# Second attention layer: one zero-finding instruction for two heads, score banks as a ring, softmax sums through a column of ones

## The chip, the cores and the metric

The kernel runs on one core of one Trainium2 chip. The metric is the device time of one execution in microseconds; times of runs are medians. The engines are named as in the profile: PE (TensorE matmul), PEld (its weight loads), DVE (VectorE), ACT (ScalarE), POOL (GpSimd) and SP (SyncE, which issues DMAs). Each engine takes its instructions in the order written, and semaphores tie the engines together.

## What is computed

Two transformer layers over x of shape 2 x 1024 x 128, each with attention and a feed-forward part, with layer norms and residual sums around each. The change touches the attention of the second layer, and the placing of scores in PSUM in both:

```
Q, K, V = split(x @ qkv.T)            # 16 heads of 8, rotary applied to Q and K
scores = Q K^T / sqrt(8)
scores = scores * lower_triangle
scores = where(scores == 0.0, -inf, scores)
attn = softmax(scores)
out = (attn @ V) @ wo.T
```

So in the second layer every score that is exactly zero is masked, which takes an instruction of its own on DVE. The first layer has 16 heads of 64 and a plain causal mask.

## The kernel before

**Items and steps.** An attention is a list of items (turn, batch, tile of 128 queries, head). In the second layer (k = 1) a turn covers 4 heads of the 16, and there are 4 turns of 64 items, 256 items in all. A turn has two halves of 32 items: batch 0 with query tiles qt = 0 to 7, then batch 1 with qt = 7 to 0, four heads of a tile after one another (a group). An item of tile qt has n = (qt + 1) * 128 keys, so 128 of the 256 items have at most 512 keys. `Attention` plans this; every engine walks the same list in a loop of its own, with these steps for item i:

- PE (`attention`, `values` in the tensor block): the scores of item i into PSUM (L1067, and L1071, which adds the causal mask); where item i - 4 ends a group, the product with V of that group (L1032), preceded by a transpose of the inverted sums (L1021); then the transposes of the probabilities of item i - 2 (L1091), for which it waits for the exponential of item i - 2. Then comes the score of item i + 1.
- DVE (`mask`, `maximum`): Zb, which is -1e30 where a score is zero (L787), then Sm, scores plus Zb with their row minimum (nmax) in one instruction and a read of the accumulator (L801). Once a group it also writes reciprocals of the sums (L769), spreads them over the columns (L776) and multiplies values by them (L759).
- ACT: the copies of the transposed probabilities PSUM to SBUF (L554), the exponential from Sm with the row sum in its accumulator (L574), and once a group a copy of the transposed factors (L536).

**PSUM.** Scores have four banks of 512 columns, as two tensors of two banks; item i writes tensor i % 2, whatever its size. Hence the score of item i waits for item i - 2 (`pe.wait_ge(a["p"] if k == 0 else a["mx"], i - 1)`).

**DMA.** SP loads Q and K of the next turn (`stacks`, 18 DMAs for each batch) once the last scores of a half are done. In the first layer the softmax factors are spread once a half turn: SP writes them to DRAM and reads them back broadcast over partitions (`spread`), and POOL multiplies 128 x 1024 values by them (L498).

**After attention** PE multiplies by wo1 (L1230, 16 tiles of 128 tokens), and norms and the last feed-forward part follow.

The steps as in the code:

```
for i in range(plan.n + QUEUED + 1):
    ... scores of i ...
    if plan.ends_group(i - QUEUED):
        values(k, plan.group(i - QUEUED), i)
    if i < plan.n + 2:
        if i >= 2:
            pe.wait_ge(a["p"], i - 1)
        ... transposes of item i - 2 ...
```

## Time and profile before

| | us |
|---|---|
| runs, median (lowest to highest) | 1345.51 (1344.99 to 1348.77) |
| the profiled execution's own time | 1347.31 |
| its span, first to last instruction | 1345.5 |
| busy: PE, DVE, ACT, POOL | 1147.0, 938.8, 850.0, 122.8 |
| first-layer attention, about | 42 to 640 |
| second-layer attention, about | 875 to 1281 |

Busy time says how much of the span an engine had an instruction at work; neighbours on one engine overlap by some tens of ns in these records, so start to start is the measure of what one costs in a row. "Idle before" names what ended the idle time of that engine.

### The profile page before, as it was taken

The page shows a single profiled execution, that of the slowest core. Times are in us where ns is not written, and L with a number is a line of the kernel's source. Part 1 is how long each engine was busy: PE and PEld are TensorE (multiplying, and loading weights), DVE is VectorE, ACT ScalarE, POOL GpSimd, SP SyncE.
Part 4 walks back from the last instruction along what each step waited for, and adds up shares of the span by engine and source line. Part 5 has one row for each costly group of instructions (what it writes and reads, how often), then busy time and mean ns, then how long its engine had stood idle before and what let it go on. Part 6 is the DMA issues. An engine that isn't in the chain of part 4 may idle for free.

```text
span 1345.5 us, 28730 instructions
## 1 busy us (share of the span) xinstructions
PE 1147.0 (85%) x10458; PEld 856.4 (64%) x10458; DVE 938.8 (70%) x2353; ACT 850.0 (63%) x1996; POOL 122.8 (9%) x105
## 2 busy tenths in 40 slices
PE   3699999989898989989989995188888888888886
PEld 1476767767676767767957773055655655656674
DVE  4466666666566666666543337589999899999953
ACT  2466666656666666665044332389989889999923
POOL 1600000000000000000400005100000000000033
PEclk9899999999999999999979997679999999999998
DMA  4212222221212222220100000422022022020001
GB/s 115 71 40 64 54 64 70 65 70 36 75 51 52 55 68 66 64 64 18 48 5 17 17 11 1 129 37 37 2 37 37 2 37 37 2 37 2 2 1 32
DMA packets 29672, 56.77 MB, mean 42 GB/s; under 512 B 4538, under 2 KB 14674, under 8 KB 29410
## 3 DMA queue, kind: packets, MB, share of 16 engines
q1 hardware_dynamic: 28738, 53.43, 17.4%
q8 instruction: 82, 1.34, 0.4%
q10 hardware_dynamic: 800, 1.57, 0.4%
q14 instruction: 52, 0.43, 0.1%
HBM read 25.49 MB, written 4.33 MB: 22 GB/s over the span
## 4 chain that ended last, share of the span: by engine, by line
PE 40%; DVE 26%; issue 18%; ACT 11%; DMA 3%; SPq 1%; POOL 1%; ACTq 0%; DVEq 0%; POOLq 0%
DVE Zb L787 9%; PE pT L1091 7%; PE pO L1032 7%; PE pS L1067 6%; ACT probs L574 4%; PE pS L1153 4%; DVE nmax L797 4%; PE pT L1165 3%; DVE Sm L801 3%; ACT PT L554 2%; PE pS L1114 2%; PE pT L994 2%; PE pT L998 2%; DVE Kl L737 1%; PE pS L1250 1%
## 5 line engine op out<-in xcount | busy, mean ns | idle before, releaser
L1091 PE MATMUL pT<-cst,probs 128*128 128x128 f32 x2304 | 374.0, 287 | 84.8 <-ACT probs L574 54.0
L1091 PEld LDWEIGHTS pT<-cst,probs 128*128 128x128 f32 x2304 | 248.9, 142 | 180.6 <-ACT probs L574 120.2
L574 ACT ACTIVATE probs<-pS,nmax 128x128 f32<-128x128 f32 (+7 forms) x256 | 190.1, 743 | 191.4 <-DVE nmax L797 157.9
L554 ACT COPY PT<-pT 128x512 f32<-128x512 f32 (+3 forms) x597 | 275.1, 483 | 12.8 <-PE pT L1091 11.3
L797 DVE TENSOR_REDUCE nmax<-pS 128x1 f32<-128x128 f32 (+7 forms) x256 | 192.1, 751 | 93.3 <-PE pS L1071 92.0
L1032 PE MATMUL pO<-PT,V 128*64 128x128 f32 (+1 forms) x4608 | 229.8, 276 | 7.9 <-issue 4.0
L574 ACT ACTIVATE probs<-Sm,nmax 128x128 f32<-128x128 f32 (+7 forms) x256 | 199.3, 778 | 28.6 <-DVE nmax L801 22.4
L787 DVE TENSOR_SCALAR Zb<-pS 128x128 bf16<-128x128 f32 (+7 forms) x256 | 192.8, 753 | 21.6 <-PE pS L1071 21.5
L1032 PEld LDWEIGHTS pO<-PT,V 128*64 128x64 f32 (+1 forms) x4608 | 179.9, 113 | 27.4 <-issue 6.5
L801 DVE CUSTOM_DVE_ANT_0 Sm<-pS,Zb 128x128 f32<-128x128 f32 (+7 forms) x256 | 193.4, 756 | 4.5
L1067 PE MATMUL pS<-Kh,Qs 128*128 128x512 f32 (+2 forms) x384 | 174.7, 459 | 7.1 <-DMA Kl<-Kl 6.9
L833 DVE COPY PT<-pT 128x512 f32<-128x512 f32 (+3 forms) x171 | 87.8, 514 | 74.0 <-PE pT L1091 70.7
L1067 PE MATMUL pS<-KS,QS 72*128 72x512 bf16 (+3 forms) x384 | 107.1, 333 | 33.2 <-DMA KS<-split 29.9
L1067 PE MATMUL pS<-Kl,Qs 128*128 128x512 f32 (+2 forms) x384 | 131.5, 346 | 0.0
L1071 PE MATMUL pS<-causalb,identb 128*128 128x128 bf16 x512 | 116.7, 228 | 0.0
L1067 PEld LDWEIGHTS pS<-Kh,Qs 128*128 128x128 f32 x384 | 75.3, 196 | 28.7 <-issue 22.9
L464 POOL TENSOR_TENSOR rstd<-rstd,power 128x4 f32<-128x4 f32 x32 | 32.8, 1025 | 622.1 <-DVE rstd L694 621.6
L498 POOL TENSOR_TENSOR attnT<-attnT,wq_t 128x1024 f32<-128x1024 f32 x16 | 37.9, 2369 | 550.0 <-DMA wq_t<-factors 505.0
L1067 PEld LDWEIGHTS pS<-Kl,Qs 128*128 128x128 f32 x384 | 74.8, 195 | 20.2 <-issue 16.0
L1071 PEld LDWEIGHTS pS<-causalb,identb 128*128 128x128 bf16 x512 | 50.4, 98 | 54.6 <-issue 33.3
L614 ACT ACTIVATE hT<-pS,b1e 128x512 f32<-128x512 f32 x64 | 43.8, 687 | 59.0 <-PE pS L1153 58.9
L994 PE MATMUL pT<-xnT,w0s 128*128 128x512 f32 x128 | 73.7, 663 | 8.5 <-DVE Ql L733 7.8
(177 smaller groups left out, 1270.9 us busy)
## 6 DMA issues: line engine op xcount, KB each, us to landing
Qs<-Ql SPq DMA_DIRECT2D x32, 256.0 KB, 3.7
Kh<-Kh SPq DMA_DIRECT2D x32, 256.0 KB, 3.6
Kl<-Kl SPq DMA_DIRECT2D x32, 256.0 KB, 4.6
wq_t<-factors SPq DMA_DIRECT2D x32, 256.0 KB, 4.0
QS<-split SPq DMA_DIRECT2D x72, 64.0 KB
KS<-split SPq DMA_DIRECT2D x72, 64.0 KB
w0s<-in_w SPq DMA_DIRECT2D x8, 192.0 KB, 4.8
split<-parts SPq DMA_DIRECT2D x2, 768.0 KB, 3.5
```

The source lines that it names most:

```text
L554: nc.scalar.copy(PT[:, g % 2, h, k0 * P:(k0 + nk) * P], pT[r % TBANKS][:, 0:nk * P])\
L574: nc.scalar.activation(probs[:, i % NPROB, 0:n], src[:, 0:n], ACT.Exp, bias=nmax[:, i % 4:i % 4 + 1], scale=sign, accum_out=total).then_in ...
L787: nc.vector.tensor_scalar(Zb[:, i % NMASK, 0:n], pS[i % 2][:, 0:n], 0.0, MASKED, ALU.is_equal, ALU.mult).then_inc(a["z"], 1)
L797: nc.vector.tensor_reduce(nmax[:, i % 4:i % 4 + 1], pS[i % 2][:, shift(k, qt):shift(k, qt) + n], AX.X, ALU.max, negate=True).then_inc(a["m ...
L801: nc.vector.tensor_tensor_reduce(Sm[:, i % NMASK, 0:n], pS[i % 2][:, 0:n], Zb[:, i % NMASK, 0:n], -(DH1 ** -0.5), 3e38, ALU.add, ALU.min, ...
L833: nc.vector.tensor_copy(PT[:, gg % 2, hh, k0 * P:(k0 + nk) * P], pT[r % TBANKS][:, 0:nk * P])\
L994: return nc.tensor.matmul(p, w0s[:, what, :], xnT[:, b * S + j * BANK:b * S + (j + 1) * BANK], start=True, stop=True)
L1032: m = nc.tensor.matmul(pO[rows, 0:P], v, PT[:, g % 2, h, kt * P:(kt + 1) * P], start=(kt == 0), stop=(kt == qt), skip_group_check=True)
L1067: nc.tensor.matmul(pS[i % 2][:, (off + c0) * P:(off + c1) * P], lhs, keys[:, b, h, c0 * P:c1 * P], start=(n == 0), stop=(n == len(rhs) - 1 ...
L1071: nc.tensor.matmul(pS[i % 2][:, (off + qt) * P:(off + qt + 1) * P], identb[:, :], causalb[:, :], start=False, stop=True).then_inc(a["s"], 1)
L1091: m = nc.tensor.transpose(pT[r % TBANKS][:, kt * P:(kt + 1) * P], probs[:, item % NPROB, (k0 + kt) * P:(k0 + kt + 1) * P], ident)
L1153: nc.tensor.matmul(bank[u % 4], w1s[:, buf, f * P:(f + 1) * P], xnT[:, j * BANK:(j + 1) * BANK], start=True, stop=True).then_inc(up_done, 1)
```

## The change

Four parts:

- `mask` runs once for two heads where n is at most 512: one instruction over 2 x n scores in two neighbouring banks. It waits until both items have their scores. Larger items keep one instruction each.
- Score banks are a ring: an item of at most 512 keys takes one bank, a larger one two, and the score of an item waits for the last item that held its banks (`place_scores`). This holds for both layers. The wait becomes i - 4 for most small items of the second layer, stays i - 2 for large ones, and is i - 2 or i - 3 in the first layer.
- V of the second layer gets a column of ones before each head's 8 columns, so that row 0 of each head's 32 rows of the output is the sum. The accumulator of the exponential, the reciprocals, the spreading copy, PE's transpose of factors and DVE's multiplication go. ACT's copy takes the values themselves, to attn1T.
- Once a half turn SP moves the sums to DRAM and back as 128 x 32, DVE inverts them (at item 16 of the next half, `invert_sums`), SP moves them out and in broadcast with four DMAs, and POOL multiplies 128 x 1024 values. PE waits for the last of these halfway through wo1.

The steps' distances stay: `lag` is 2 for both layers, so the transposes of item i - 2 still come in step i.

```diff
+        self.lag, self.queued, self.nprob = lag, lag + 2, lag + 1
...
+    def place_scores(self):
+        self.bank_of, self.after, last, at = [], [], [-1] * 4, 0
+        for i, (_, _, qt, _) in enumerate(self.items):
+            size = -(-(qt + 1) * P // BANK)
+            at = 0 if at + size > 4 else at
+            self.bank_of.append(at)
+            self.after.append(max(last[at:at + size]))
+            last[at:at + size] = [i] * size
+            at = (at + size) % 4
...
+    def masks(self, i):
+        if self.items[i][2] >= TPB:
+            return 1
+        return 2 if i % 2 == 0 else 0
...
+        V1 = at(32, "V1", [P, NT, HEADS, DH1 + 1])
+        rsb1 = at(42, "rsb1", [P, S])
+        sums = at(46, "sums", [P, HPG * S // P])
...
+            def spread1(half):
+                g, b = divmod(half, B)
+                sp.wait_ge(A[1]["n"], (half + 1) * ST)
+                sp.dma_start(sums_row[half, :, :], attn1T[0:P:HEAD_ROWS, b, g, :]).then_inc(sums_out, 16)
+                sp.wait_ge(sums_out, 16 * (half + 1))
+                sp.dma_start(sums[:, :], sums_row[half, :, :].rearrange("h (j i) -> (h j) i", i=HPG * S // P)).then_inc(sums_in, 16)
+                sp.wait_ge(sums_inverted, half + 1)
+                sp.dma_start(factors1[half, :, :].rearrange("h (j i) -> (h j) i", i=HPG * S // P), sums[:, :]).then_inc(factors1_out, 16)
+                sp.wait_ge(factors1_out, 16 * (half + 1))
+                if half >= 1:
+                    sp.wait_ge(rescaled1, half)
+                for h in range(HPG):
+                    sp.dma_start(rsb1[h * HEAD_ROWS:h * HEAD_ROWS + DH1 + 1, :],
+                                 factors1[half, h:h + 1, :].to_broadcast([DH1 + 1, S])).then_inc(factors1_in, 16)
...
+            for half in range(G1 * B):
+                values = attn1T[:, half % B, half // B, :]
+                pool.wait_ge(factors1_in, 16 * HPG * (half + 1))
+                pool.tensor_tensor(values, values, rsb1[:, :], ALU.mult).then_inc(rescaled1, 1)
...
+            def values_out(a, g):
+                c, b, qt = L[1].order[g]
                 act.wait_ge(a["o"], g + 1)
-                nc.scalar.copy(rs[:, g % 2, :], pO[:, P:2 * P]).then_inc(a["rs"], 1)
+                nc.scalar.copy(attn1T[:, b, c, qt * P:(qt + 1) * P], pO[:, 0:P]).then_inc(a["n"], 1)
...
                 def mask(i):
-                    n = (plan.items[i][2] + 1) * P
-                    dve.wait_ge(a["s"], i + 1)
+                    n, heads = (plan.items[i][2] + 1) * P, plan.masks(i)
+                    dve.wait_ge(a["s"], i + heads)
                     if i >= NMASK:
-                        dve.wait_ge(a["p"], i - NMASK + 1)
+                        dve.wait_ge(a["p"], i - NMASK + heads)
...
+                    half, at_half = divmod(i, plan.per // B)
+                    if k == 1 and at_half == 16 and half >= 1:
+                        invert_sums(half - 1)
...
-                        if i >= 2:
-                            pe.wait_ge(a["p"] if k == 0 else a["mx"], i - 1)
+                        if plan.after[i] >= 0:
+                            pe.wait_ge(a["p"] if k == 0 else a["mx"], plan.after[i] + 1)
...
-                    if i < plan.n + 2:
-                        if i >= 2:
-                            pe.wait_ge(a["p"], i - 1)
+                    if i < plan.n + plan.lag:
+                        if i >= plan.lag:
+                            pe.wait_ge(a["p"], i - plan.lag + 1)
...
+            pe.wait_ge(rescaled1, G1 * B - 1)
             for n in range(NT):
+                if n == ST:
+                    pe.wait_ge(rescaled1, G1 * B)
```

Order on DVE in the second layer, where items of 256 keys give way to 384, before (Zb and Sm are written from the scores pS; a1_s counts scores done, a1_p exponentials, a1_z masks):

```order
L787 TENSOR_SCALAR Zb<-pS 128x384 [waits a1_p,a1_s]
L759 TENSOR_TENSOR attn1T<-pO,rs 128x128 [waits a1_rs]
L801 ISA Sm,nmax<-pS,Zb 128x384 [waits a1_z]
L801 ISA nmax 128x1
L787 TENSOR_SCALAR Zb<-pS 128x384 [waits a1_p,a1_s]
L769 RECIPROCAL rden<-den 128x4 [waits a1_p]
L801 ISA Sm,nmax<-pS,Zb 128x384 [waits a1_z]
L801 ISA nmax 128x1
L776 COPY rdb<-rden 128x128 [waits a1_rd1]
```

and with the change, at the same place:

```order
L836 TENSOR_SCALAR Zb<-pS 128x2x384 [waits a1_p,a1_s]
L849 ISA Sm,nmax<-pS,Zb 128x384 [waits a1_z]
L849 ISA nmax 128x1
L849 ISA Sm,nmax<-pS,Zb 128x384 [waits a1_z]
L849 ISA nmax 128x1
L836 TENSOR_SCALAR Zb<-pS 128x2x384 [waits a1_p,a1_s]
```

One Zb stands ahead of two Sm, and waits for two scores; the three once-a-group instructions are gone.

Order on PE at that place with the change (a1_mx counts Sm done, a1_cp_act ACT's copies; pT holds transposes):

```order
L1113 MATMUL pS<-KS,QS 128x384 [waits a1_mx]
L1117 MATMUL pS<-causalb,identb 128x128
L1137 MATMUL pT<-cst,probs_77 128x128 [waits a1_cp_act,a1_p]
L1137 MATMUL pT<-cst,probs_77 128x128
L1113 MATMUL pS<-KS,QS 128x384 [waits a1_mx]
L1117 MATMUL pS<-causalb,identb 128x128
L1137 MATMUL pT<-cst,probs_77 128x128 [waits a1_cp_act,a1_p]
L1137 MATMUL pT<-cst,probs_77 128x128 x2
```

It is the order of before (there L1067, L1071, L1091, with the same waits): between the scores of two items stand the transposes of an earlier one, which wait for an exponential. What moved is only the count of a1_mx that a score waits for.

## Rows read from the trace of the kernel before

**Rows 1.** The page: the span.

```profile
span 1345.5 us, 28730 instructions
```

**Rows 2.** Stretches: PE, PEld, DVE, ACT, POOL busy, PEclk, DMA share, GB/s.

```profile
900.00:1000.00 100.00, 85.51 (x1048) 59.72 (x1047) 97.63 (x242) 92.62 (x242) 0.00 (x0) 1.00 0.19 25
975.00:980.00 5.00, 3.68 (x48) 2.27 (x45) 4.42 (x29) 4.71 (x24) 0.00 (x0) 1.00 0.27 45
```

**Rows 3.** Groups by form, 875 to 1285 us: busy us, mean ns | idle before.

```profile
L787 DVE TENSOR_SCALAR Zb<-pS 128x1024 bf16<-128x1024 f32 x32 | 39.0, 1219 | 0.0
...
L574 ACT ACTIVATE probs<-Sm,nmax 128x512 f32<-128x512 f32 x32 | 23.4, 733 | 2.9 <-DVE nmax L801 1.3 <-PE pT L1091 0.9
L801 DVE CUSTOM_DVE_ANT_0 Sm<-pS,Zb 128x512 f32<-128x512 f32 x32 | 22.0, 689 | 0.6
...
L787 DVE TENSOR_SCALAR Zb<-pS 128x256 bf16<-128x256 f32 x32 | 13.5, 421 | 1.6 <-PE pS L1071 1.5
L574 ACT ACTIVATE probs<-Sm,nmax 128x128 f32<-128x128 f32 x32 | 12.9, 404 | 0.7 <-issue 0.2
```

**Rows 4.** Timeline, 990 to 992 us, 512 keys: start, duration, engine, line.

```profile
990.07 0.72 ACT L574 ACTIVATE probs<-Sm,nmax 128x512 f32<-128x512 f32 x1 [0.28 <-PE pT L1091]
...
990.70 0.19 ACT L574 ACTIVATION_READ_ACCUMULATOR probs<-Sm,nmax 128x1 f32 x1
...
990.94 0.66 PE L1091 MATMUL pT<-cst,probs 128*128 128x128 f32 x4 [0.48 <-ACT probs L574]
991.21 0.08 DVE L801 DVE_READ_ACCUMULATOR2_ANT nmax<- 128x1 f32 x1
...
991.38 0.72 ACT L574 ACTIVATE probs<-Sm,nmax 128x512 f32<-128x512 f32 x1
...
991.65 0.22 PE L1071 MATMUL pS<-causalb,identb 128*128 128x128 bf16 x1
```

**Rows 5.** Timeline, 1271 to 1278 us, 256 and 128 keys.

```profile
1271.37 0.22 PE L1071 MATMUL pS<-causalb,identb 128*128 128x128 bf16 x1
...
1271.63 0.42 DVE L787 TENSOR_SCALAR Zb<-pS 128x256 bf16<-128x256 f32 x1 [0.19 <-PE pS L1071]
...
1276.94 0.33 PE L1091 MATMUL pT<-cst,probs 128*128 128x128 f32 x1
...
1277.16 0.22 PE L1071 MATMUL pS<-causalb,identb 128*128 128x128 bf16 x1
```

**Rows 6.** Timeline of DVE: first Zb of 512 keys down, first of 640 up.

```profile
960.59 0.69 DVE L787 TENSOR_SCALAR Zb<-pS 128x512 bf16<-128x512 f32 x1
...
994.01 0.82 DVE L787 TENSOR_SCALAR Zb<-pS 128x640 bf16<-128x640 f32 x1
```

**Rows 7.** Timeline of DVE, items of 1024 keys.

```profile
919.24 1.22 DVE L801 CUSTOM_DVE_ANT_0 Sm<-pS,Zb 128x1024 f32<-128x1024 f32 x1
...
924.17 1.22 DVE L801 CUSTOM_DVE_ANT_0 Sm<-pS,Zb 128x1024 f32<-128x1024 f32 x1
...
926.58 1.23 DVE L801 CUSTOM_DVE_ANT_0 Sm<-pS,Zb 128x1024 f32<-128x1024 f32 x1
...
929.06 1.22 DVE L801 CUSTOM_DVE_ANT_0 Sm<-pS,Zb 128x1024 f32<-128x1024 f32 x1
```

**Rows 8.** Groups by form, 100 to 600 us, first layer: a score's matmul.

```profile
L1067 PE MATMUL pS<-Kh,Qs 128*128 128x512 f32 x129 | 68.1, 528 | 0.0
```

**Rows 9.** Line 971 on DVE: ns min/median/max, both operands in SBUF.

```profile
L971 DVE TENSOR_TENSOR rot<-rot x4: 1212/1217/3285, 836.5 to 856.8; 128x1024 f32<-128x1024 f32 x4
```

**Rows 10.** Timeline of SP and of POOL at the first layer's last half.

```profile
639.05 0.31 SPq L379 DMA_DIRECT2D factors<-factorsT  x1
640.45 1.08 SPq L386 DMA_DIRECT2D wq_t<-factors  x2
...
645.02 2.35 POOL L498 TENSOR_TENSOR attnT<-attnT,wq_t 128x1024 f32<-128x1024 f32 x1 [17.19 <-DMA wq_t<-factors]
```

**Rows 11.** Chain that ended last, 1270 us to the end.

```profile
1280.97 16.19 PE pS L1230 x128
```

More of the change, by code:

```diff
@@ L55 @@
 STACK = PARTS * PARTS * DH1
+HEAD_ROWS = P // HPG
 KIB = 1024
@@ L133, in order_for_dve, with scores @@
             self.done_by[step]["dve"] = count
+    def place_scores(self):
[7 more added lines that the diff above has]
+            at = (at + size) % 4
+        self.masked_by, count = [], 0
+        for i in range(self.n):
+            count += self.masks(i) > 0
+            self.masked_by.append(count)
+    def masks(self, i):
+        if self.items[i][2] >= TPB:
+            return 1
+        return 2 if i % 2 == 0 else 0
+    def scores(self, pS, i, k0, nk):
+        start = self.bank_of[i] * BANK + k0
+        return pS[:, start:start + nk]
     def project(self, step, c, b, u):
@@ L560, in exponential @@
                         n, g = (qt + 1) * P, plan.group(i)
-                        if i >= NPROB:
-                            act.wait_ge(a["t"], plan.round_of[i - NPROB] + 1)
+                        if i >= plan.nprob:
+                            act.wait_ge(a["t"], plan.round_of[i - plan.nprob] + 1)
                         half, at_half = divmod(i, plan.per // B)
+                        if k == 0 and half >= 2 and at_half == 0:
+                            act.wait_ge(dens_inverted, half - 1)
@@ L573, in exponential @@
-                        src, sign = (pS[i % 2][:, shift(k, qt):], 1.0) if k == 0 else (Sm[:, i % NMASK, :], -1.0)
-                        nc.scalar.activation(probs[:, i % NPROB, 0:n], src[:, 0:n], ACT.Exp,
-                                             bias=nmax[:, i % 4:i % 4 + 1], scale=sign,
-                                             accum_out=total).then_inc(a["p"], 1)
-                for i in range(plan.n + QUEUED + 1):
-                    if k == 1 and plan.ends_group(i - QUEUED):
-                        factors_out(a, plan.group(i - QUEUED))
+                            nc.scalar.activation(probs(k, i)[:, 0:n], plan.scores(pS, i, shift(k, qt), n), ACT.Exp,
+                                                 bias=nmax[:, i % 4:i % 4 + 1],
+                                                 accum_out=den0[:, half % 2, h, qt:qt + 1]).then_inc(a["p"], 1)
+                        else:
+                            nc.scalar.activation(probs(k, i)[:, 0:n], Sm[:, i % NMASK, 0:n], ACT.Exp,
+                                                 bias=nmax[:, i % 4:i % 4 + 1], scale=-1.0).then_inc(a["p"], 1)
@@ L581, in attention @@
+                for i in range(plan.n + plan.queued + 1):
+                    if k == 1 and plan.ends_group(i - plan.queued):
+                        values_out(a, plan.group(i - plan.queued))
                     if k == 0:
@@ L744, in copy_turned, with invert_sums, attention @@
                 nc.vector.tensor_copy(factorsT[:, :], pO[0:HPC * ST, P:2 * P]).then_inc(turned_copied, 1)
-            def attention(k, put):
+            def invert_sums(half):
+                dve.wait_ge(sums_in, 16 * (half + 1))
+                nc.vector.reciprocal(sums[:, :], sums[:, :]).then_inc(sums_inverted, 1)
+            def attention(k):
                 a, plan = A[k], L[k]
@@ L818, in attention @@
                         maximum(i)
-                    if summed:
-                        spread(plan.group(i - 2))
+                    half, at_half = divmod(i, plan.per // B)
+                    if k == 1 and at_half == 16 and half >= 1:
+                        invert_sums(half - 1)
                     for r in plan.dve_at[i]:
@@ L975, in _ @@
             nc.vector.memset(pO[:, 0:P], 0.0).then_inc(pO_cleared, 1)
-            attention(1, lambda g, b, qt: attn1T[:, b, g, qt * P:(qt + 1) * P])
+            nc.vector.memset(rsb1[:, :], 0.0)
+            nc.vector.memset(V1[:, :, :, 0:1], 1.0).then_inc(pO_cleared, 1)
+            attention(1)
+            invert_sums(G1 * B - 1)
             norm_stage(3, y_tile, y_ready(3))
@@ L1018, in values @@
                     turn(g // ST - 1)
-                if k == 1:
-                    pe.wait_ge(a["rd"], g + 1)
-                    nc.tensor.transpose(pO[:, P:2 * P], rdb[:, g % 2, :], ident)
-                for e2, done in plan.done_by[i - QUEUED + 2].items():
+                for e2, done in plan.done_by[i - plan.queued + plan.lag].items():
                     if done:
@@ L1037, in attention @@
                 a, plan = A[k], L[k]
-                for i in range(plan.n + QUEUED + 1):
+                for i in range(plan.n + plan.queued + 1):
                     if i < plan.n:
@@ L1276 @@
     wo1 = np.zeros((HPG, P // HPG, G1, D), np.asarray(L1_attn_wo).dtype)
-    wo1[:, 0:DH1] = np.asarray(L1_attn_wo).T.reshape(G1, HPG, DH1, D).transpose(1, 2, 0, 3)
+    wo1[:, 1:DH1 + 1] = np.asarray(L1_attn_wo).T.reshape(G1, HPG, DH1, D).transpose(1, 2, 0, 3)
     arrays = {
```

118 lines of the change are left out of this document (50 added, 68 removed).

## The prediction

> **What bounds the kernel now.** I read the page first. The span is 1345.5 us [rows 1]; the profiled execution took 1347.31 us, 1.8 us more than its span, and the median of the runs is 1345.51 us. The sums below are made against 1347.31, and the result is then taken 1.8 us lower, to stand against the median. What a measurement of this kernel can tell from no change is about 0.3%, or 4 us.
>
> Second, the stretches. In a 100 us stretch of the second layer's attention DVE is busy 97.63, ACT 92.62 and PE 85.51 [rows 2]. So DVE sets the pace there, ACT is close behind, and PE has slack. The change takes work from DVE and from ACT, which sounds like a gain. But less work on the engine that sets the pace helps only while the inputs of its next instruction are there when it comes to it. So the third view is the timeline, for how long the path takes from one Sm through ACT and PE back to a Zb.
>
> That path exists because of the order on PE: between two scores stand the transposes of the item two back, and these wait for its exponential. Now let i be even. The merged Zb of items i and i + 1 needs the score of i + 1. On PE that score stands behind the transposes of i - 2, these wait for the exponential of i - 2, and that one for Sm of i - 2. Before the change Zb of item i needed only the score of i, which stands behind the transposes of i - 3. The ring lets a score start earlier as far as banks go (wait i - 4 in place of i - 2), yet it doesn't change what stands ahead of it in PE's queue. **The merged instruction therefore asks for a score one step sooner than PE's order gives it.**
>
> **Part 1, the merged zeros, small items.** With 512 keys, from the end of Sm of i - 2:
>
> - To the exponential's start 0.09: the accumulator read ends at 991.21 + 0.08, the exponential starts at 991.38 [rows 4].
> - The exponential 0.73 [rows 3]. Its own accumulator read, which ends 0.10 after it (990.70 + 0.19 against 990.07 + 0.72) [rows 4], goes.
> - To the first transpose 0.05 (990.89 to 990.94) [rows 4].
> - Four transposes, the score and the causal matmul 0.93 (990.94 to 991.65 + 0.22) [rows 4].
> - To Zb 0.04 (1271.37 + 0.22 to 1271.63) [rows 5].
> - The merged Zb has 2 x 512 columns, and Zb of 1024 took 1.22 [rows 3]. To Sm 0.04, estimated as the gap before.
> - Sm of i, 0.69 [rows 3], and the circle is closed.
>
> That is 3.79 us for two items. With 128 keys it is 0.09 + 0.40 + 0.05 + 0.44 (1276.94 to 1277.16 + 0.22) + 0.04 + 0.42 + 0.04 + 0.29 = 1.77 us; 0.40 is the exponential of 128, 0.42 is Zb of 256 [rows 3, 5], and 0.29 is that less 128 columns at (1.22 - 0.42)/768 us each. Every piece grows evenly with the columns, so 256 and 384 keys lie between, and the four sizes take 4 x (1.77 + 3.79)/2 = 11.1 us for a pair of each. A turn has four pairs of each size: 44.5 us. DVE works in this circle for Zb and two Sm and waits for the rest: with 512 keys Sm of i - 1 fills 0.61 of the 1.84 us between Sm of i - 2 and Zb.
>
> Before, the same eight groups of a turn took 994.01 - 960.59 = 33.4 us [rows 6], with DVE hardly waiting. So the small items cost 11.1 us more in a turn, and in four turns **+44.3 us**. The bounds: the path has eight pieces read to some 0.02 us, of which the two waits and the length of the exponential without its sum are the least known. I allow 0.25 us a pair, which is 16 us over 64 pairs either way.
>
> The wait of the merged Zb for exponential i - 3 in place of i - 4 costs nothing: that of i - 2 is already in the path.
>
> **Part 2, what leaves DVE and ACT, large items.** With over 512 keys Zb stays single, and DVE keeps the pace. A group of 1024 keys took 929.06 - 919.24 = 9.82 us, and an item with none of the group's extras between 926.58 - 924.17 = 2.41, so four take 9.64 [rows 7]. A group gains 0.18 us, since two of the extras stood in the gap between Zb and Sm and only filled it. 32 groups give **-5.8 us**; the bounds are 0, and the whole busy time of the three, which I estimate at 0.6 us a group or 19 us. I take the measured start-to-start. In small items the removed work frees an engine that waits anyway, so nothing more is gained there. The shorter exponential takes load from ACT, behind DVE: nothing. PE loses a transpose a group: nothing, in its slack.
>
> **Part 3, the ring in the first layer.** For half of its items a score may now start before exponential i - 2. PE was never idle before a score of the first layer: 0.0 us before 129 of them [rows 8]. What waits there is the transposes that follow, for the same semaphore. I take 0; the bounds are -5 us (a wait shifted behind a score) and 0, since no wait becomes stricter.
>
> **Part 4, the sums by way of DRAM.** Seven of eight spreads lie beside the next half. DVE meets its wait for them at item 16; at a turn's end SP first issues 18 loads, and eight small pairs of part 1 take over 22 us meanwhile. That covers the loads and two short transfers of 1.4 us each (639.05 to 640.45 [rows 10]). If the cover went, each turn would wait what is missing, with all of PE and ACT behind DVE. The last spread is bare. SP's transfer out 1.4, in again 1.4 (the nearest row; it may be 3), the inversion 0.3 as an estimate, out 1.4, the broadcast until POOL starts 4.6 (640.45 to 645.02), POOL 2.35 [rows 10]: 11.5 us from the last values. PE meets the wait halfway through 16.19 us of wo1 [rows 11], after 8.1. **+3.4 us**, between 1 and 8; the upper end holds a slower transfer in, and POOL, whose first power of the norm now queues behind this multiplication and comes some 4.6 us later, about as late as PE. ACT's direct copy saves 0.3 us at the end, where a copy on ACT and a multiplication on DVE stood in a row. The two new memsets lie beside DVE's wait for the first K and Q.
>
> POOL's multiplications also run beside DVE. One DVE instruction with both operands in SBUF took 3.3 us in place of 1.2 at its slowest [rows 9], at a time when POOL was at work. Sm has one operand in PSUM and one in SBUF, so 0 to 8 x 2.1 = 17 us. I take 0: a POOL multiplication of the same size runs all through the first layer, where DVE reads PSUM, and no such outlier is in the rows of its lines. The Trainium skill (SBUF — State Buffer, section "SBUF: two separate sides") has it that GpSimd and VectorE lock a port pair against each other for a whole instruction, on VectorE's side when it has two SBUF inputs or runs a two-port mode. By that rule Sm is free and the sum stays; were Sm counted too, the sum would be 17 us higher. Rows 9 agree with the lock, and no row of before shows Sm beside POOL.
>
> **The sum:** +44.3 - 5.8 + 0 + 3.4 - 0.3 = +41.6 us. 1347.3 + 41.6 = 1388.9 for the profiled execution, and 1387 us against the median.
>
> **The rivals.**
>
> 1. *Faster: the merged Zb finds its scores ready.* Then DVE stays the bound. A pair of 512 keys costs 1.22 + 0.04 + 2 x 0.61 = 2.48, one of 128 keys 0.42 + 0.04 + 2 x 0.21 = 0.88, on average 1.68; 16 pairs a turn make 26.9 against 33.4. That is -26 us, and with parts 2 and 4 -28.7: **1317 us**. It turns on the path from Sm of i - 2 to the second score being shorter than Sm of i - 1, 0.61 us with 512 keys; the rows give 1.84. It needs a PE order other than the one shown. Chance 0.05.
> 2. *Slower still: PE's clock falls in the small items.* PE would idle more. The granted clock was 1.00 (2.4 GHz) with PE busy 3.68 of 5 us in 128-key items [rows 2], and I expect about that share. If it fell to 1.2 GHz, the PE piece (0.44 to 0.93, mean 0.69) could double: 64 x 0.69 = 44 us at most, half of it if the clock is low half of the time, **1409 us**. Chance 0.10.
> 3. *Sm is held up by POOL* in all eight halves: +17, **1404 us**. Chance 0.05.
> 4. *The change gives nothing* (the ring lets PE's queue get ahead enough to hide most of the path, and a part of rival 1's gain comes in). At 0.5 us less waiting a pair it is 1355, and no change needs 0.65. Chance 0.04, half of that within 0.3%.
>
> **How the numbers follow.** The forecast has 0.76. Its own range takes 16 us either way for part 1 and 5 us either way for parts 2 to 4: 1366 to 1408. The range is stretched to 1410, to hold rivals 2 and 3 at their likely sizes; rival 1 is left out. Faster: rival 1 and a little of rival 4, 0.05. Same: 0.02. Slower: the rest, 0.93.
>
> **What would show it.** In the changed profile, Zb on DVE has some 60 idle times of about 1 us ended by PE's causal matmul, 1.2 us with 512 keys and less below: some 60 us in all, where the rows of before show 0.0 to 1.6 us for each form [rows 3]. DVE's busy time in the small items falls to about two thirds. From the first Zb of 512 keys down to the first Zb of 640 up it takes 44 us, where it was 33.4. A group of 1024 keys takes 9.6 us, and PE waits some 3 us in wo1 for POOL. I am wrong if Zb hardly waits for PE in the small items, if DVE waits for a DMA at item 16, or if the first layer's length moves by more than 4 us.

## The result, and the profile after

The changed kernel takes **1400.41 us**, the median of four runs (1397.59 to 1405.27), against 1346.32 us for the kernel before in four runs beside it. The ratio is 1.0393, interval 1.0363 to 1.0423: some 54 us slower. Forecast were 1387 us and slower, with 1366 to 1410 as the range. The profiled execution took 1397.78 us.

The page of the changed kernel, span and busy time, against [rows 1]:

```profile
span 1396.0 us, 28048 instructions
PE 1171.8 (84%) x10394; PEld 864.3 (62%) x10394; DVE 917.2 (66%) x2107; ACT 829.6 (59%) x1740; POOL 141.7 (10%) x113
```

The stretches, with the columns of [rows 2]: start:end, length, then busy time and instructions of PE, PEld, DVE, ACT and POOL, then the granted clock of PE, DMA share, GB/s. First the same 100 us as in [rows 2]. Then the small items of one turn, from the first Zb of 512 keys down to the first Zb of 640 up. Then the same 5 us as in [rows 2], and the whole second layer's attention.

```profile
900.00:1000.00 100.00, 81.64 (x955) 55.82 (x952) 83.72 (x163) 80.67 (x163) 2.35 (x1) 0.92 0.18 24
965.45:1013.90 48.45, 35.44 (x309) 22.28 (x310) 27.98 (x82) 28.23 (x74) 2.35 (x1) 0.70 0.20 29
975.00:980.00 5.00, 4.69 (x45) 3.33 (x46) 2.03 (x7) 3.16 (x8) 0.00 (x0) 0.50 0.01 3
875.00:1328.00 453.00, 368.79 (x4087) 248.58 (x4085) 365.24 (x711) 348.69 (x703) 16.49 (x7) 0.87 0.16 23
```

The same small items of the kernel before, between the two Zb of [rows 6]:

```profile
960.59:994.01 33.42, 27.84 (x325) 18.36 (x324) 31.63 (x121) 31.38 (x108) 0.00 (x0) 1.00 0.28 35
```

They grew from 33.42 to 48.45 us (46.86 and 47.18 in the two other whole turns). DVE's share of them fell from 95% to 58%: no engine is full there any more. PE looks 73% busy, but that is at a mean clock of 0.70. Where the clock stands at 0.50, PE has 4.69 of 5 us busy and still does less (45 matmuls against 48 in [rows 2]).

The groups of DVE by form, 875 to 1330 us: busy us, mean ns | idle before, and what ended it. They answer to [rows 3].

```profile
L836 DVE TENSOR_SCALAR Zb<-pS 128x1024 bf16<-128x1024 f32 x48 | 58.6, 1221 | 19.7 <-PE pS L1117 19.7
L836 DVE TENSOR_SCALAR Zb<-pS 128x768 bf16<-128x768 f32 x48 | 45.8, 955 | 23.6 <-PE pS L1117 23.6
L836 DVE TENSOR_SCALAR Zb<-pS 128x896 bf16<-128x896 f32 x32 | 34.8, 1086 | 0.0
...
L849 DVE CUSTOM_DVE_ANT_0 Sm<-pS,Zb 128x512 f32<-128x512 f32 x32 | 20.9, 681 | 0.5
```

Of the 48 Zb with 1024 columns 16 are merged ones (pairs of 512 keys), of those with 768 columns 16 are pairs of 384. The idle time sits ahead of these forms, while 896 columns, which no pair has, show 0.0. Over all forms it is 88.8 us, where it was 21.6. Both hold the wait for the attention's very first score, 9.1 and 10.6 us, so the waits inside it grew from 11 to 79.7 us:

```profile
L836 DVE TENSOR_SCALAR Zb<-pS 128x768 bf16<-128x768 f32 (+5 forms) x192 | 183.2, 954 | 88.8 <-PE pS L1117 88.8
```

Now the circle itself (the chain in which each step waits for the one before it, and the first for the last), one pair of 512 keys in the timeline of all engines: start, duration, engine and line, then the operation, and in brackets the idle time before it.

```profile
965.45 1.22 DVE L836 TENSOR_SCALAR Zb<-pS 128x1024 bf16<-128x1024 f32 x1 [0.68 <-PE pS L1117]
...
966.71 0.69 DVE L849 CUSTOM_DVE_ANT_0 Sm<-pS,Zb 128x512 f32<-128x512 f32 x1
...
967.50 0.72 ACT L632 ACTIVATE probs<-Sm,nmax 128x512 f32<-128x512 f32 x1 [1.17 <-DVE nmax L849]
...
968.28 0.66 PE L1137 MATMUL pT<-cst,probs 128*128 128x128 f32 x4 [1.46 <-ACT probs L632]
...
968.99 0.22 PE L1117 MATMUL pS<-causalb,identb 128*128 128x128 bf16 x1
...
969.25 1.23 DVE L836 TENSOR_SCALAR Zb<-pS 128x1024 bf16<-128x1024 f32 x1 [1.02 <-PE pS L1117]
```

Zb, Sm, the exponential, the transposes, the score behind them in PE's queue, the next Zb: each starts within 0.1 us of the end of the one before it. From Zb to Zb it is 3.80 us; the forecast from pieces of the old trace was 3.79. The stretch of this pair, with its clock (1.00), and one of 512 keys in which PE ran at half of that:

```profile
965.45:969.25 3.80, 2.05 (x17) 1.38 (x21) 2.74 (x7) 2.63 (x7) 0.00 (x0) 1.00 0.03 4
...
1006.00:1013.90 7.90, 6.21 (x45) 3.96 (x44) 5.07 (x11) 3.58 (x8) 0.00 (x0) 0.50 0.01 2
```

```profile
1006.30 1.22 DVE L836 TENSOR_SCALAR Zb<-pS 128x1024 bf16<-128x1024 f32 x1 [1.76 <-PE pS L1117]
...
1010.81 1.22 DVE L836 TENSOR_SCALAR Zb<-pS 128x1024 bf16<-128x1024 f32 x1 [1.94 <-PE pS L1117]
```

1010.81 - 1006.30 = 4.51 us, 0.71 more than 3.80. DVE's 1.22 and the exponential's 0.72 stay; the difference is PE's part.

Last the end of the attention, against [rows 10] and [rows 11]: the sums' way through DRAM, and PE's wait in the middle of wo1.

```profile
1329.94 0.51 SPq L477 DMA_DIRECT2D sums_row<-attn1T  x1
...
1331.78 0.35 SPq L479 DMA_DIRECT2D sums<-sums_row  x1
1333.57 0.35 DVE L806 RECIPROCAL sums<-sums 128x32 f32<-128x32 f32 x1 [6.55 <-DMA sums<-sums_row]
...
1338.83 2.34 POOL L566 TENSOR_TENSOR attn1T<-attn1T,rsb 128x1024 f32<-128x1024 f32 x1 [24.33 <-DMA rsb<-factors]
...
1341.23 7.41 PE L1279 MATMUL pS<-wo1s,attn1T 128*128 128x128 f32 x64 [2.52 <-POOL attn1T L566]
```

Where the 50.5 us between the spans are: wo1 starts at 1329.97 in place of 1280.97 [rows 11], +49.0, while the second layer's first Sm starts within 0.4 us of the same time, 875.55 before and 875.9 now. Behind that start it is +1.5. In the attention the small items of all four turns took 189.6 us in place of 136.7, the large ones 262.0 in place of 266.1.

### The profile page after: what moved, and what is told of

Read it like the earlier page. It is cut to its first block, busy times and chain, and to the rows that moved or that the text cites. A ratio compares the mean times of both kernels' runs of the same rounds, so it can differ in the third digit from the quotient of the medians.

```text
span 1396.0 us, 28048 instructions
## 1 busy us (share of the span) xinstructions
PE 1171.8 (84%) x10394; PEld 864.3 (62%) x10394; DVE 917.2 (66%) x2107; ACT 829.6 (59%) x1740; POOL 141.7 (10%) x113
## 4 chain that ended last, share of the span: by engine, by line
PE 44%; DVE 24%; issue 17%; ACT 11%; DMA 2%; POOL 1%; SPq 1%; ACTq 0%; POOLq 0%; DVEq 0%
PE pT L1137 10%; DVE Zb L836 9%; PE pO L1078 8%; PE pS L1113 7%; PE pS L1199 4%; DVE nmax L845 4%; PE pT L1211 3%; ACT probs L632 3%; PE pS L1160 2%; PE pT L1047 2%; ACT PT L614 2%; PE pT L1043 2%; DVE Kl L795 1%; ACT probs L628 1%; PE pS L1117 1%
## 5 line engine op out<-in xcount | busy, mean ns | idle before, releaser
L1137 PE MATMUL pT<-cst,probs 128*128 128x128 f32 x2304 | 389.2, 295 | 109.5 <-ACT probs L632 79.3
L1137 PEld LDWEIGHTS pT<-cst,probs 128*128 128x128 f32 x2304 | 256.7, 146 | 211.4 <-ACT probs L632 124.3
L1078 PE MATMUL pO<-PT,V 128*64 128x128 f32 (+1 forms) x4608 | 238.6, 286 | 7.6 <-issue 3.2
L836 DVE TENSOR_SCALAR Zb<-pS 128x768 bf16<-128x768 f32 (+5 forms) x192 | 183.2, 954 | 88.8 <-PE pS L1117 88.8
L849 DVE CUSTOM_DVE_ANT_0 Sm<-pS,Zb 128x128 f32<-128x128 f32 (+7 forms) x256 | 188.9, 755 | 6.6
L1113 PE MATMUL pS<-KS,QS 72*128 72x512 bf16 (+3 forms) x384 | 117.6, 362 | 32.9 <-DMA KS<-split 29.7
L1117 PE MATMUL pS<-causalb,identb 128*128 128x128 bf16 x512 | 121.8, 238 | 0.0
L1117 PEld LDWEIGHTS pS<-causalb,identb 128*128 128x128 bf16 x512 | 53.5, 104 | 58.4 <-issue 34.9
L991 DVE SCALAR_TENSOR_TENSOR acc<-pT,wcol,acc 128x128 f32<-128x128 f32 x96 | 27.0, 344 | 64.3 <-PE pT L1211 64.3
```

Source lines behind the costliest of these rows:

```text
L836: nc.vector.tensor_scalar(to, source, 0.0, MASKED, ALU.is_equal, ALU.mult).then_inc(a["z"], 1)
L849: nc.vector.tensor_tensor_reduce(Sm[:, i % NMASK, 0:n], plan.scores(pS, i, 0, n), Zb[:, i % NMASK, 0:n], -(DH1 ** -0.5), 3e38, ALU.add, AL ...
L1078: m = nc.tensor.matmul(pO[rows, 0:P], v, PT[:, g % 2, h, kt * P:(kt + 1) * P], start=(kt == 0), stop=(kt == qt), skip_group_check=True)
L1113: nc.tensor.matmul(plan.scores(pS, i, (off + c0) * P, (c1 - c0) * P), lhs, keys[:, b, h, c0 * P:c1 * P], start=(n == 0), stop=(n == len(rh ...
L1117: nc.tensor.matmul(plan.scores(pS, i, (off + qt) * P, P), identb[:, :], causalb[:, :], start=False, stop=True).then_inc(a["s"], 1)
L1137: m = nc.tensor.transpose(pT[r % TBANKS][:, kt * P:(kt + 1) * P], probs(k, item)[:, (k0 + kt) * P:(k0 + kt + 1) * P], ident)
```

## The experiments

My theory: the merged Zb waits for a score that stands in PE's queue behind transposes, that circle sets the pace of the small items, and the part of the loss above the forecast is PE's clock. The rivals: the circle is right but the clock costs nothing; the ring or the way of the sums costs it; DVE or PE work, and no chain, sets the pace. All ten kernels start from the changed one and compute the whole result. The ratio is to the kernel before, run beside each; its median was 1347.39 us beside runs 1 to 4, 1346.05 beside runs 5 to 8 and 1347.99 beside runs 9 and 10, and its single times lay between 1338 and 1354 us. "Small items" is the stretch of one turn used above. The last two columns add up the whole attention of the profiled execution, from the first Zb to the end of the last Sm, start to start: all stretches of small items, and the four stretches of large items between them.

| kernel | median us | ratio, interval | small items us | all small | all large |
|---|---|---|---|---|---|
| before | 1346.32 | 1 | 33.42 | 136.7 | 266.1 |
| changed | 1400.41 | 1.0393, 1.0363 to 1.0423 | 48.45 | 189.6 | 262.0 |
| 1 both scores first | 1353.44 | 1.0048, 1.0022 to 1.0073 | 33.03 | 137.5 | 267.0 |
| 2 transposes one later | 1375.01 | 1.0201, 1.0176 to 1.0226 | 39.85 | 158.6 | 265.7 |
| 3 zeros one by one | 1350.88 | 1.0018, 0.9988 to 1.0048 | 31.50 | 129.5 | 274.1 |
| 4 no ring | 1399.88 | 1.0389, 1.0368 to 1.0409 | 46.48 | 188.1 | 261.6 |
| 5 dummies for the clock | 1387.00 | 1.0316, 1.0278 to 1.0354 | 43.39 | 176.2 | 263.4 |
| 6 exp's sum put back | 1406.58 | 1.0444, 1.0417 to 1.0470 | 49.91 | 197.4 | 264.9 |
| 7 one by one, sums later | 1334.98 | 0.9931, 0.9908 to 0.9953 | 31.35 | 128.8 | 258.8 |
| 8 both scores, sums later | 1347.93 | 1.0017, 0.9997 to 1.0036 | 34.58 | 140.3 | 258.8 |
| 9 as 7, exp's sum | 1343.07 | 0.9961, 0.9940 to 0.9983 | 32.30 | 131.0 | 259.7 |
| 10 as 7, no ring | 1339.79 | 0.9927, 0.9900 to 0.9953 | 31.41 | 129.8 | 260.3 |

**1. Both scores first.** PE issues the scores of both items of a pair ahead of the transposes of i - 2.

```
-                    if i < plan.n:
-                        (score of item i)
+                    if i < plan.n and (k == 0 or plan.masks(i)):
+                        score(i)
+                        if k == 1 and plan.masks(i) == 2:
+                            score(i + 1)
```

> The changed kernel, with one thing moved: on PE the scores of both items of a merged pair stand in a row, ahead of the transposes of item i - 2. Path theory (the merged Zb waits because the second score stands behind those transposes): the circle Sm, exponential, transposes, score, Zb is one item longer now, so it covers more. A pair of 512 keys should take 2.5 (DVE alone) to 2.8 us in place of 3.8, one of 128 keys 0.9 to 1.3 in place of 1.8, and the small items of a turn 27 to 33 us in place of 47: 1320 to 1345 us, and idle before Zb falls from 89 us to under 35. Rival (the merged instruction is slow by itself, or the clock does it): no more than 10 us are gained, 1390 or above.

The circle opened: the small items fell from 48.45 to 33.03 us and 47 of the 54 us came back, by this order on PE alone. But the time stayed above what I expected, for two reasons. Zb still waited for PE: 38.4 us in all (11.3 of it for the first score), where I expected under 35. And DVE now came to the sums of the half before too early:

```profile
992.64 0.35 DVE L806 RECIPROCAL sums<-sums 128x32 f32<-128x32 f32 x1 [2.41 <-DMA sums<-sums_row]
```

It did so at two of the three turn ends, for 2.41 and 3.42 us, beside the bare wait of 6.04 us after the last half.

**2. Transposes one item later.** The other way to open it: the transposes of i - 3, not i - 2, stand behind the score of i.

```
-        L = [Attention(HPC, CH0, ["act", "dve"], True, 2), Attention(HPG, G1, ["act"], False, 2)]
+        L = [Attention(HPC, CH0, ["act", "dve"], True, 2), Attention(HPG, G1, ["act"], False, 3)]
-        probs1 = at(136, "probs1", [P, 3, S])
+        probs1 = at(136, "probs1", [P, 4, S])
```

> The changed kernel with a distance of 3 in the second layer: transposes of item i - 3 in step i, values one step later, four buffers for probabilities. Path theory: the second score of a pair stands behind the transposes of i - 3, whose exponential is the second of the pair before; at 512 keys that path (about 2.4 us) is under DVE's own 2.5 us, at 128 keys about 1.05 against 0.88. Small items of a turn 28 to 32 us, 1318 to 1335 us in all, faster than the kernel before. Rival (merging costs by itself): 1390 or above.

Half of the loss stayed. Zb now waits, nearly always, before every second pair only (DVE's timeline):

```profile
998.95 1.22 DVE L836 TENSOR_SCALAR Zb<-pS 128x1024 bf16<-128x1024 f32 x1 [2.15 <-PE pS L1117]
...
1001.43 1.22 DVE L836 TENSOR_SCALAR Zb<-pS 128x1024 bf16<-128x1024 f32 x1
```

and PE has a new wait, for ACT's copies that free the three banks of the transposes (waits, 875 to 1340 us: total us, times, longest):

```profile
DVE Zb L836 <- PE pS L1117: 66.5, 41, 11.9
...
PE pT L1137 <- ACT PT L614: 33.4, 57, 2.0
```

(The 66.5 us hold the 11.9 for the first score.) In the changed kernel no transpose waited for those copies, and the weight loads ahead of them for 3.3 us in all. The clock fell here too: it stood at a mean of 0.83 in the small items, where the kernel before had 1.00.

```profile
964.06:1003.91 39.85, 28.98 (x309) 19.82 (x307) 27.35 (x80) 26.80 (x72) 2.36 (x1) 0.83 0.25 35
```

How much of the 28 us that stayed is the wait for the copies and how much the clock was not separated, and I didn't try whether a fourth bank would free this order.

**3. Zeros one by one.** The merge alone undone; ring, column of ones and spread kept.

```
     def masks(self, i):
-        if self.items[i][2] >= TPB:
-            return 1
-        return 2 if i % 2 == 0 else 0
+        return 1
```

> The changed kernel with the zeros of every item found by an instruction of its own, as before; ring and sums by DRAM stay. Path theory: the whole loss lies in the merging, so what is left is the gain of the other parts: 5.8 us in large items, some 10 us in small ones where DVE set the pace, less 2 to 3 us for the last spread: 1330 to 1338 us. Rival (the ring or the sums cost something in the loop): above 1346.

The loss went with the merge: 1350.88 against 1347.39 us beside it, and the ratio's interval holds 1. The small items took 31.50 us, less than before the change, yet 1330 to 1338 was not reached, for the reason seen in run 1, larger (DVE's timeline at a turn's end):

```profile
991.17 0.82 DVE L834 TENSOR_SCALAR Zb<-pS 128x640 bf16<-128x640 f32 x1
...
996.88 0.35 DVE L804 RECIPROCAL sums<-sums 128x32 f32<-128x32 f32 x1 [4.02 <-DMA sums<-sums_row]
...
1003.44 0.96 DVE L834 TENSOR_SCALAR Zb<-pS 128x768 bf16<-128x768 f32 x1 [1.45 <-PE pS L1115]
```

DVE waited 4.02, 2.39 and 4.15 us at the three turn ends, 10.6 us in all. The wait goes on to the other engines: PE stood idle for 4.23 us ahead of its next score, and its clock, 1.00 in the small items before, had a mean of 0.72 over this stretch.

```profile
991.17:1003.44 12.27, 7.18 (x63) 4.39 (x62) 6.67 (x16) 6.11 (x13) 1.26 (x1) 0.72 0.17 29
```

**4. No ring.** Two pairs of banks in turn, in both layers; the merged Zb reads them with a stride.

```
-            size = -(-(qt + 1) * P // BANK)
-            at = 0 if at + size > 4 else at
+            size, at = 2, i % 2 * 2
...
-            at = (at + size) % 4
```

> The changed kernel without the ring: item i writes the first or second pair of banks again and waits for item i - 2, in both layers; the merged Zb reads two banks that are 1024 columns apart. Path theory: the banks don't bind, since the score stands behind the transposes in any case; within 4 us of the changed kernel (1396 to 1405). The first layer, 2 us shorter with the ring, gets them back. Rival (the ring brought PE ahead in the small items, or its bank order costs time there): more than 8 us either way.

1399.88 against 1400.41 us: in the changed kernel the ring neither costs nor saves anything that shows. What I expected of the first layer did not come: its last factors left for DRAM at 633.48 us without the ring, earlier than the changed kernel's 636.99 with it, not later.

**5. Dummies for the clock.** While PE would wait for the exponential it transposes the identity into the bank that the real transposes then overwrite.

```
+                        if k == 1 and 2 <= i < plan.n and plan.masks(i) == 2:
+                            r = plan.at_step[i][0]
+                            if r >= TBANKS:
+                                pe.wait_ge(a["cp_act"], plan.rounds[r - TBANKS][2]["act"])
+                            for _ in range(2 * (plan.items[i][2] + 1)):
+                                nc.tensor.transpose(pT[r % TBANKS][:, 0:P], ident, ident)
```

> Adds to the changed kernel, in every pair of small items of the second layer, 2 to 8 dummy transposes (2 times the key tiles) into the transposes' bank that the next real transposes overwrite; the results are the same. They run while PE would wait for the exp. Theory (part of the loss over the predicted 44 us is the fallen PE clock: a 512 pair took 3.80 us at a granted clock of 1.00 and 4.51 at 0.50): PE is busier in the small items, the clock stays near 1.00 there, pairs take 3.8, 3.1, 2.5 and 1.8 us, the small stretches between the large items go from 47 back to about 45 us or below, and the time falls from 1400 to 1388 to 1394. Rival (the clock is no cause, or the dummies are in the way of the real transposes): the granted clock rises but the time stays at 1398 or above.

More work on PE made the kernel 13 us faster. The same stretch of this kernel has the clock at 1.00 throughout, and DVE's busy time is as it was (27.89 against 27.98 us):

```profile
964.24:1007.63 43.39, 34.03 (x380) 24.09 (x378) 27.89 (x82) 26.41 (x71) 2.36 (x1) 1.00 0.25 33
```

Two pairs of it, of 128 keys and of 512:

```profile
984.63 0.42 DVE L836 TENSOR_SCALAR Zb<-pS 128x256 bf16<-128x256 f32 x1 [0.82 <-PE pS L1117]
986.43 0.43 DVE L836 TENSOR_SCALAR Zb<-pS 128x256 bf16<-128x256 f32 x1 [0.82 <-PE pS L1117]
...
1001.34 1.23 DVE L836 TENSOR_SCALAR Zb<-pS 128x1024 bf16<-128x1024 f32 x1 [1.15 <-PE pS L1117]
1005.14 1.23 DVE L836 TENSOR_SCALAR Zb<-pS 128x1024 bf16<-128x1024 f32 x1 [1.23 <-PE pS L1117]
```

1.80 and 3.80 us a pair, where the forecast had 1.77 and 3.79. With the clock held the kernel takes 1387.00 us, and the traces put the gain where the dummies are: all small items took 176.2 us in place of 189.6, 13.4 less, and the large ones 263.4 in place of 262.0.

**6. The exponential's sum put back.** A dose on ACT, to see whether the path runs over it.

```
                             nc.scalar.activation(probs(k, i)[:, 0:n], ..., ACT.Exp,
-                                                 bias=..., scale=-1.0).then_inc(a["p"], 1)
+                                                 bias=..., scale=-1.0,
+                                                 accum_out=unused[:, i % 4:i % 4 + 1]).then_inc(a["p"], 1)
```

> A dose for the path: every exp of the second layer writes its sum again (to a place that nobody reads), which costs ACT about 0.1 us an item; the rest is the changed kernel. Theory (in the small items the circle Sm, exp, transposes, scores, merged zeros is what the pair lasts, and the exp stands on it once or twice a pair; in the large items DVE sets the pace): 64 small pairs times 0.1 to 0.2 us, 6 to 13 us slower than the changed kernel, 1406 to 1413, all of it in the small items. Rival (DVE or PE work sets the pace there too, ACT has air): no change, 1398 to 1402.

+6.2 us by the medians, near the low end: 64 pairs times 0.1. The profiled execution was the slowest of six, 1413.06 us; in it the small items took 7.8 us more than in the changed kernel and the large ones 2.9, so "all of it in the small items" is not borne out to the microsecond. A pair of 512 keys went from 3.80 to 3.89 us, at a clock of 1.00 in both:

```profile
969.86 1.23 DVE L838 TENSOR_SCALAR Zb<-pS 128x1024 bf16<-128x1024 f32 x1 [0.79 <-PE pS L1119]
...
973.75 1.23 DVE L838 TENSOR_SCALAR Zb<-pS 128x1024 bf16<-128x1024 f32 x1 [1.12 <-PE pS L1119]
```

ACT, busy 28 of 48 us there, is on the path once a pair.

**7. One by one, and the sums inverted later.**

```
-                    if k == 1 and at_half == 16 and half >= 1:
+                    if k == 1 and at_half == 24 and half >= 1:
```

> Ring and sums of the change kept, zeros found one item at a time, and DVE's inversion of a half turn's sums moved from item 16 of the next half to item 24. With item 16 this took 1351 us and DVE waited 10.6 us for the sums' transfer. Theory (after the small items ran at the old pace, the sums were asked for too early, and what DVE waited there was lost): no wait for the sums, the large stretches fall from 70 to 65 us, 12 to 16 us in all, 1334 to 1341, faster than the kernel before (1346). Rival (the wait only took the place of another one): 1347 to 1352.

As the theory had it: 16 us less than run 3 by the medians (12 by the ratios) by this one number, and **faster than both kernels**, 1334.98 against 1346.05 us, 0.7% with an interval clear of 1. In the traces the large stretches fell from 274.1 to 258.8 us, 15.3 less. DVE's own waits at the turn ends had been 10.6 of them. The rest fits what run 3's trace shows behind such a wait, a late score (1.45 us) and a lower clock, though no run takes the two apart. DVE's only wait for the sums is now the bare one after the last half (groups, 875 to 1340 us), and DVE is full again:

```profile
L804 DVE RECIPROCAL sums<-sums 128x32 f32<-128x32 f32 x8 | 2.8, 348 | 5.9 <-DMA sums<-sums_row 5.9
```

```profile
957.56:988.91 31.35, 26.52 (x317) 17.55 (x316) 29.60 (x100) 28.87 (x76) 2.36 (x1) 1.00 0.30 40
900.00:1000.00 100.00, 86.31 (x1057) 59.13 (x1061) 97.08 (x200) 90.60 (x184) 2.36 (x1) 1.00 0.21 28
```

**8. Both scores first, sums later** (the edits of runs 1 and 7).

> Merged zeros with both score products of a pair issued ahead of the transposes that stood between them, ring, and the inversion of the sums at item 24. With item 16 this took 1353 us, of it 11.9 us in DVE's waits for the sums. Theory: the large stretches fall from 65 to 70 to 65 us, 1339 to 1344; beside the one-by-one kernel with the same sums it tells what the merged zeros are worth once their circle is shortened: at 38 against 20 us of idle time ahead of the zeros and 0.1 us a pair saved, 3 to 8 us slower than that. Rival (the merged zeros pay once nothing else is in the way): faster than the one-by-one kernel, below 1335.

1347.93, 4 us above what I expected, and 13 above run 7: even with its circle opened, the merged Zb costs. In the traces the large items took the same 258.8 us as in run 7, and the small ones 140.3 in place of 128.8. The expectation itself had an error: it counted on all 11.9 us of run 1's waits for the sums, but 6.0 of them are the bare wait after the last half, which item 24 can't hide (6.19 us here). The other 5.8 went, and the median fell by 5.5. The small items did not get shorter. At their end, where run 1 waited 0.16 us for PE, it is now

```profile
1000.56 0.82 DVE L836 TENSOR_SCALAR Zb<-pS 128x640 bf16<-128x640 f32 x1 [1.72 <-PE pS L1116]
```

**9. Run 7 with the exponential's sum** (the edits of runs 3, 7 and 6).

> The fastest kernel so far (zeros one by one, ring, sums from the column of ones, inverted at item 24: 1335 us) with the sum written again by every exp of the second layer. Theory (with the zeros one by one ACT's part counts only where DVE, which now works over 93 of 100 us, waits for it: in some small items): 31.5 us a turn of small items go back to 33 at most, 0 to 6 us slower, 1335 to 1341. Rival (ACT stands on the path in every small pair here too, as in the changed kernel, where the same dose cost 6 us in 64 pairs): 1341 to 1345, and then the gain over the kernel before is mostly the sum that the exps no longer write.

By its median, 1343.07 us, it falls into the rival's range: +8 us. But the ratios say +0.3% (4 us) with intervals that overlap, and in the traces all small items took 131.0 us in place of 128.8 and the large ones 259.7 in place of 258.8, while 6.7 us more had passed before the second layer's attention began, which has no part in the edit. So the sum costs some 3 to 4 us here by the traces and ratios, inside what the theory had allowed; the runs don't settle it closer.

**10. Run 7 without the ring** (the edits of runs 3, 7 and 4).

> The same kernel with the score banks of the kernel before in both layers (two pairs of banks in turn) in place of the ring. Theory (PE gets scores into a bank pair two items back, and the third bank ahead never decides): the same time as with the ring, 1333 to 1338. Rival (the ring lets PE run further ahead of DVE in the small items once the merge is away): 1339 or above, with idle time ahead of the zeros above 16 us.

By its median, 1339.79 us, it is 4.8 us above run 7 and just inside the rival's range, and Zb's waits for PE were 18.7 us, above the 16 that the rival named (16.1 in run 7). By the ratio it is the same (0.9927 against 0.9931), as the kernel before was itself 2 us slower beside this run. In the traces the attention took 2.5 us more (129.8 and 260.3 against 128.8 and 258.8). So the ring may be worth some 2 us once the merge is gone; four runs don't show it.

## Why the prediction was right, and where it was not

- **Part 1, the circle.** Right in its mechanism (runs 1, 3, 5, 6) and in the size of its pieces: at the full clock 3.80 and 1.79 us a pair against 3.79 and 1.77. Sixteen pairs were put at 44.5 us; with the clock held they took 43.39, because the last pair runs only until a single Zb of 640, which needs no second score (1007.63 - 1005.14 = 2.49 us). Over four turns the term came out smaller than forecast all the same: 176.2 - 136.7 = 39.5 us with the clock held, where the sum had 44.3. The other part of the difference is that the first and the last stretch of small items took 19.6 + 16.8 us before the change, 3 us more than the 33.4 put for them.
- **The mis-sized term: the clock.** The forecast took PE's clock as 1.00 in the small items and left its fall to rival 2, with a chance of 0.10. The step was "The granted clock was 1.00 (2.4 GHz) with PE busy 3.68 of 5 us in 128-key items [rows 2], and I expect about that share". The pair of 512 keys shows that PE did not keep that share: it was busy 2.05 of 3.80 us. Ahead of the fall it had been busy 5.77 of 8.75 us at a clock of 1.00, in a chain with waits of over a microsecond, where the kernel before had 27.84 of 33.42; then the clock stood at 0.50 (1.2 GHz):

```profile
965.45:974.20 8.75, 5.77 (x71) 4.01 (x71) 6.45 (x13) 5.79 (x13) 1.61 (x1) 1.00 0.08 20
```

  It rose again at about 981 us, in the pairs of 256 keys, and fell again at about 991.5, at the end of those of 128; what in PE's work decides this, the runs don't show. Run 5 puts the price at 13 us, 13.4 by the medians and 13.4 by the small items of the traces. Rival 2 said 22 for the clock low half of the time; the mean of 0.70 in that stretch is low for 60% of it, but a pair lost at most 0.71 us (4.51 against 3.80), where rival 2 allowed 0.93 with 512 keys: PE's piece there grew from 0.93 to 1.65 us (1009.12 to 1010.46 + 0.31, first transpose to the end of the causal matmul) and did not double. So the outcome lies between the forecast and rival 2: the forecast's mechanism, with a part of the rival's on top.
- **The sum.** That run 5 gives the forecast's 1387 us is in part luck. By the traces the changed kernel lost 52.9 us in the small items, gained 4.1 in the large ones, and lost 1.5 behind the attention and 0.2 before it; with the clock held the small items lose 39.5, not 44.3, and the gain in the large items is not the one forecast (part 2).
- **The idle time ahead of Zb.** "Some 60 us in all": without the first score's wait 79.7 with the fallen clock, 68.4 in run 5. DVE's share of the small items, "about two thirds", was 58%, and 64% in run 5.
- **Part 2.** A group of 1024 keys took 932.61 - 922.99 = 9.62 us, forecast 9.64:

```profile
922.99 1.22 DVE L836 TENSOR_SCALAR Zb<-pS 128x1024 bf16<-128x1024 f32 x1
...
932.61 1.22 DVE L836 TENSOR_SCALAR Zb<-pS 128x1024 bf16<-128x1024 f32 x1
```

  The total of -5.8 us was not seen, though. The large stretches took 65.73 us in three turns before the change and 68.91 in the second, which held one wait of 3.08 us for a score; with the change they took 64.91 to 66.25, and in run 5, at a clock of 1.00, 65.71 to 65.91. Of the 1.4 us a turn up to 1.5 went again, because the last large item is followed by the first merged Zb, which already waits for two scores (it waited 0.68 us in the changed kernel, 1.49 in run 5). Only one by one did the gain come: 64.14 to 65.36 us in run 7.

- **Part 3.** Right: run 4 gives 1399.88 us without the ring. The first layer's last factors left for DRAM 2.1 us earlier (639.05 [rows 10], now 636.99), inside the 4 us allowed, but that isn't the ring's doing: this time lies between 630.63 (run 1) and 639.69 (run 6) in kernels with the same first layer, and at 633.48 and 635.95 in the two without the ring. The second layer began no earlier for it.
- **Part 4, the bare spread.** Forecast 11.5 us from the last values to the end of POOL's multiplication; measured from the end of PE's last values (1329.60) to 1338.83 + 2.34, 11.6 us. PE waited 2.52 us in wo1 for "some 3", and behind the start of wo1 the kernel lost 1.5 us where the sum had 3.4. The 0.3 us ahead of wo1 didn't show: from the last Sm's start to wo1 it was 3.2 us in both.
- **Part 4, the cover.** "If the cover went, each turn would wait what is missing, with all of PE and ACT behind DVE" held, and cost more than what was missing. In the changed kernel the cover stood, and of DVE's 6.5 us for the sums all was in the last half. It went as soon as the small items were fast again: 15 us over three turn ends in the traces of runs 3 and 7. The forecast had rested the cover on the slow pairs ("eight small pairs of part 1 take over 22 us meanwhile"); what the expectation of run 3 left out is that with them the cover goes, so undoing the merge alone does not show its price.
- **POOL beside Sm**, rival 3. Seven of POOL's eight multiplications ran while DVE was still at the attention, the first from 972.59 to 974.94 beside an Sm of 384 keys of the usual 0.56 us. Over all 256 Sm the longest is 1225 ns, as in the kernel before, whose POOL was idle there:

```profile
L849 DVE CUSTOM_DVE_ANT_0 Sm<-pS,Zb x256: 285/758/1225, 875.9 to 1326.7; 128x128 f32<-128x128 f32 x16, 128x256 f32<-128x256 f32 x16, 128x384 f32<-128x384 f32 x16, 128x512 f32<-128x512 f32 x16
```

  Taking 0 there was right. By the Trainium skill (SBUF — State Buffer, section "SBUF: two separate sides") the lock needs two SBUF inputs or a two-port mode on VectorE, and Sm has one of its two inputs in PSUM; the trace agrees (1225 ns at most).
- **Rival 1** would have needed another order on PE than the change has. Run 1 had that order, and its small items took 33.03 us, not 26.9: even then the second score was late, and Zb waited for PE 27.1 us in 40 places, the attention's first score not counted.

## What to carry to other kernels

Before two instructions are merged, look in the producer's queue at what stands ahead of the second input: a merged instruction needs the later of its inputs, and if transposes that wait for the consumer's own result stand between them, the merge closes a circle. Add the circle up from the pieces of the old trace, then look whether the matrix engine comes to wait in it where it was busy before, and price its slower clock as part of the forecast. And when a transfer is hidden, note what hides it: a fix that makes the cover shorter can need the wait moved at the same time, as between runs 3 and 7. A count of waits is not what moving them gives back: a bare one stays (run 8), and a hidden one can return more than its length (run 7).

## What the hardware showed that I had not expected

- PE's granted clock fell to 0.50 with PE waiting in a chain, and with 2 to 8 dummy transposes a pair it stayed at 1.00 in the whole turns. A pair of 512 keys at full clock took 3.80 us with and without them, and the kernel gained 13 us.
- Kernels that agree in the first layer began the second layer's attention up to 9.9 us apart in their profiled executions (871.27 us in run 1, 881.20 in run 9; 874.51 in run 7). PE's clock was 1.00 in run 7 and 0.97 in run 9 in a stretch where PE had no idle time (run 7 first, then run 9):

```profile
700.00:800.00 100.00, 100.00 (x588) 73.93 (x587) 34.41 (x136) 38.12 (x56) 0.00 (x0) 1.00 0.05 15
```

```profile
700.00:800.00 100.00, 100.00 (x549) 71.59 (x549) 32.80 (x130) 38.49 (x56) 0.00 (x0) 0.97 0.05 15
```

  A difference of a few us between two kernels is therefore read from the stretch that the edit touches, and from many runs.
